# Three-layer graph network and a mixture of experts on one core: the bias products of the experts padded to 128 rows, z loaded back in 13 transfers, the mean negated on Pool

## The reference

```python
x = x + gnn(layernorm(x), edges)          # x is 10000 x 512, 20000 directed edges and loops
x = x + moe(layernorm(x))
# gnn, three layers:
agg = segment_sum(x[src], dst) / max(deg, 1)
out = agg @ Wl + bl + x @ Wr;  x = where(out >= 0, out, a * out)
# moe, 8 experts of 64 hidden columns, the two best of each row:
cw = top2(softmax(x @ Wr + br))
out = sum over e of cw[:, e] * (relu(x @ W1[e] + b1[e]) @ W2[e] + b2[e])
```

## Time and profile before

| | |
|---|---|
| median of 3 runs | 2628.05 us (2627.36 to 2632.61) |
| the profiled execution | 2626.7 us |
| its span | 2624.9 us |
| mean granted clock of TensorE | 0.996 |
| TensorE busy | 2570.3 us (98%) |
| weight loads busy | 1629.7 us (62%) |
| VectorE busy | 1908.0 us (73%) |
| ScalarE busy | 1486.6 us (57%) |
| Pool busy | 1037.5 us (40%) |

### The profile page before, as it was taken

How to read it: one execution, slowest core, us unless ns; L and a number is a source line. 1 busy time by engine, 2 the same in 40 slices (tenths; PEclk the granted TensorE clock), 3 DMA queues, 4 the chain that set the end, 5 groups by cost and what they waited for, 6 DMA issues and landing times.

```text
span 2624.9 us, 40317 instructions
## 1 busy us (share of the span) xinstructions
PE 2570.3 (98%) x9906; PEld 1629.7 (62%) x9906; DVE 1908.0 (73%) x5137; ACT 1486.6 (57%) x3471; POOL 1037.5 (40%) x1291
## 2 busy tenths in 40 slices
PE   7999999999999999999999999999999999999999
PEld 3444445555588865555488874545457777777776
DVE  5555555555699965555599975577579998899996
ACT  2232245555388855555288875555436565556655
POOL 2222245554244445555233325555323333333331
PEclk9999999999999999999999999999999999999999
DMA  4343368887355458888445449988623235223221
GB/s 132 132 134 130 129 206 266 272 267 252 100 165 164 165 186 279 265 270 267 136 152 165 164 155 324 327 283 264 211 73 96 91 93 189 94 87 91 93 89 61
DMA packets 207839, 460.65 MB, mean 175 GB/s; under 512 B 34689, under 2 KB 35001, under 8 KB 207672
## 3 DMA queue, kind: packets, MB, share of 16 engines
q0 software_dynamic: 64928, 207.55, 27.0%
q1 hardware_dynamic: 73480, 124.92, 13.5%
q10 hardware_dynamic: 69264, 126.12, 13.0%
HBM read 245.06 MB, written 213.93 MB: 175 GB/s over the span
## 4 chain that ended last, share of the span: by engine, by line
PE 93%; DVE 2%; DMA 1%; issue 1%; ACT 1%; SPq 0%; POOL 0%; another core or an unknown queue 0%; ACTq 0%; DVEq 0%; POOLq 0%
PE psY L670 11%; PE psY L788 9%; PE psM L788 9%; PE psH L788 8%; PE psY L684 6%; PE psY L692 6%; PE psY L701 5%; PE psT L650 5%; PE psS L800 4%; PE psS L801 4%; PE psY L875 3%; PE psY L878 3%; PE psH L922 3%; PE psH L909 3%; PE psY L887 3%; PE psH L913 3%
## 5 line engine op out<-in xcount | busy, mean ns | idle before, releaser
L559 POOL DMA_INDIRECT rows<-y_rows,lists x471 | 490.7, 1042 | 465.1 <-PE psS L801 304.1
L1323 DVE TENSOR_TENSOR lows<-rows,highs 128x512 fp32r<-128x512 f32 x471 | 326.2, 693 | 354.6 <-ACT highs L956 319.9
L956 ACT ACTIVATE outs<-psS 128x512 f32<-128x512 f32 x471 | 279.6, 594 | 277.2 <-PE psS L801 235.4
L956 ACT ACTIVATE highs<-rows 128x512 fp32r<-128x512 f32 x471 | 294.8, 626 | 144.5 <-ACT outs L956 92.2
L800 PE MATMUL psS<-highs,sel 128*128 128x512 f32 x471 | 346.1, 735 | 11.2 <-ACT outs L956 7.7
L566 POOL DMA_INDIRECT rows<-sum_rows,nodeI x158 | 210.6, 1333 | 314.5 <-DVE rows L1331 299.8
L670 PE MATMUL psY<-wy,res 128*128 128x512 f32 x632 | 285.8, 595 | 0.7 <-ACT res L956 0.7
L956 ACT ACTIVATE outs<-psY 128x512 f32<-128x512 f32 x237 | 141.8, 599 | 223.5 <-PE psY L670 213.7
L788 PE MATMUL psM<-wz,res 128*128 128x512 f32 x544 | 255.5, 592 | 0.0
L788 PE MATMUL psY<-wz,res 128*128 128x512 f32 x536 | 251.7, 592 | 0.0
L788 PE MATMUL psH<-wz,res 128*128 128x512 f32 x528 | 248.0, 592 | 0.0
(11 more groups left out here) (202 smaller groups left out, 4940.6 us busy)
## 6 DMA issues: line engine op xcount, KB each, us to landing
sum_rows<-outs ACTq DMA_DIRECT2D x471, 256.0 KB
y_rows<-outs SPq DMA_DIRECT2D x237, 256.0 KB
rows<-in_x POOLq DMA_DIRECT2D x78, 256.0 KB, 3.0
outs<-in_x SPq DMA_DIRECT2D x78, 256.0 KB
out_rows<-res SPq DMA_DIRECT2D x78, 256.0 KB, 2.0
rows<-y_rows,lists POOLq DMA_INDIRECT x471
z_rows<-res SPq DMA_DIRECT2D x13, 512.0 KB
res<-z_rows SPq DMA_DIRECT2D x1, 6656.0 KB, 24.1
```

The source lines that it names most:

```text
L559: pool.indirect_dma_start(out=rows[:, t % RING, :], out_offset=None, in_=y_d, in_offset=bass.IndirectOffsetOnAxis(ap=col(srcT, t), axis=0) ...
L956: act.activation(o, i_, ACT.Copy).then_inc(signal, 1)
L1323: dve.tensor_tensor(lows[:, t % RING, :], rows[:, t % RING, :], highs[:, g, :].bitcast(F32), ALU.subtract)\
```

## The change

- `twos` and `b1s` get 128 rows. b1 is loaded to all 128 rows by one broadcast transfer instead of two one-row ones. `twos` is one in rows 0 and 1 and zero elsewhere, by way of the new column `two_rows`; `b1s` is zero from row 2 on.
- `cwT` and `b2s` get 128 rows. Pool fills them with zeros once, after the last scatter of the last layer; SyncE's load of b2 and ScalarE's first `norm` wait for it (`pad_set`). Later writes touch rows 0 to 31 alone.
- `bring_back` becomes 13 transfers of two tiles each, one at each k from 30 to 42; piece j waits for j + 1 stores of each of the two slots. VectorE waits for all 13.
- VectorE no longer negates the mean (L1522); Pool's shift becomes mean times reciprocal root times -1 in one operation.

```diff
-        cwT = nc.alloc_sbuf_tensor_at("cwT", [4 * X, 2, P], F32R, offset=lists_at)
+        cwT = nc.alloc_sbuf_tensor_at("cwT", [P, 2, P], F32R, offset=lists_at)
-        twos = nc.alloc_sbuf_tensor_at("twos", [2, P], F32R, offset=res_at + 48 * D + 4 * P)
-        b1s = nc.alloc_sbuf_tensor_at("b1s", [2, D], F32R, offset=res_at + 52 * D)
-        b1raw, b1high = res[0:2, 24, :], res[0:2, 25, :]
+        twos = nc.alloc_sbuf_tensor_at("twos", [P, P], F32R, offset=res_at + 48 * D + 4 * P)
+        b1s = nc.alloc_sbuf_tensor_at("b1s", [P, D], F32R, offset=res_at + 52 * D)
+        b1raw, b1high = res[:, 24, :], res[:, 25, :]
+        two_rows = res[:, 12, 2 * P:2 * P + 1]
-        b2s = nc.alloc_sbuf_tensor_at("b2s", [4 * X, D], F32R, offset=hw_at + 8 * D)
+        b2s = nc.alloc_sbuf_tensor_at("b2s", [P, D], F32R, offset=hw_at + 8 * D)
...
-                for k in range(2):
-                    sp.dma_start(b1raw[k:k + 1, :], b1.rearrange("e f -> (e f)").unsqueeze(0)).then_inc(ex_in, 16)
+                load_row(b1raw, b1.rearrange("e f -> (e f)"), ex_in)
...
                     sp.wait_ge(b2_st, 16)
-                    sp.dma_start(b2s[:, :].bitcast(F32), b2_d).then_inc(b2_back, 16)
+                    sp.wait_ge(pad_set, 2)
+                    sp.dma_start(b2s[0:4 * X, :].bitcast(F32), b2_d).then_inc(b2_back, 16)
...
-            def bring_back():
+            def bring_back(j):
                 for s in range(2):
-                    sp.wait_ge(o_st[s], 16 * (AWAY // 2))
-                sp.dma_start(res[:, AWAY:2 * AWAY, :], z_d.rearrange("(t p) d -> p t d", p=P)).then_inc(z_back, 16)
+                    sp.wait_ge(o_st[s], 16 * (j + 1))
+                a = 2 * j
+                sp.dma_start(res[:, AWAY + a:AWAY + a + 2, :], z_d[a * P:(a + 2) * P].rearrange("(t p) d -> p t d", p=P))\
+                  .then_inc(z_back, 16)
...
-                if k == AWAY + 8:
-                    bring_back()
+                j = k - AWAY - 4
+                if 0 <= j < AWAY // 2:
+                    bring_back(j)
...
+                if l + 1 == LAYERS:
+                    pool.memset(cwT[:, :, :].bitcast(F32), 0.0).then_inc(pad_set, 1)
+                    pool.memset(b2s[:, :].bitcast(F32), 0.0).then_inc(pad_set, 1)
                 pool.wait_ge(mend_st, 32 * (l + 1))
...
-                pool.tensor_tensor(st[:, s, SHIFT:SHIFT + 1], st[:, s, MEAN:MEAN + 1], st[:, s, RSTD:RSTD + 1],
-                                   ALU.mult).then_inc(shift_in[s], 1)
+                pool.tensor_scalar(st[:, s, SHIFT:SHIFT + 1], st[:, s, MEAN:MEAN + 1], st[:, s, RSTD:RSTD + 1], -1.0,
+                                   ALU.mult, ALU.mult).then_inc(shift_in[s], 1)
...
-                copy(cwT[:, s, :], psS[1][0:4 * X, 0:P], cw_sb[s])
+                copy(cwT[0:4 * X, s, :], psS[1][0:4 * X, 0:P], cw_sb[s])
...
             act.wait_ge(mend_add, 2 * LAYERS)
+            act.wait_ge(pad_set, 2)
...
-                dve.tensor_scalar(twos[:, :], iota[0:2, :], 0.0, None, ALU.is_ge).then_inc(ex_set, 1)
+                link(dve.tensor_tensor(two_rows, ident[:, 0:1], ident[:, 1:2], ALU.add))
+                dve.tensor_scalar(twos[:, :], iota[:, :], 0.0, two_rows, ALU.is_ge, ALU.mult).then_inc(ex_set, 1)
...
-                        dve.wait_ge(z_back, 16)
+                        dve.wait_ge(z_back, 16 * (AWAY // 2))
...
-                    dve.tensor_scalar(stat(MEAN), stat(MEAN), -1.0, None, ALU.mult)
```

More of the change, by code:

```diff
@@ L287, in build @@
         cw_made = sem("cw_made")
+        pad_set = sem("pad_set")
         block = ctx.enter_context(nc.Block())
@@ L434, in _ @@
             sp.wait_ge(b2_set, 1)
-            sp.dma_start(b2_d, b2s[:, :].bitcast(F32)).then_inc(b2_st, 16)
+            sp.dma_start(b2_d, b2s[0:4 * X, :].bitcast(F32)).then_inc(b2_st, 16)
             def load_own(k):
@@ L1207, in split_b2 @@
                 link(dve.tensor_scalar(b2raw, b2raw, is_low, None, ALU.mult))
-                dve.scalar_tensor_tensor(b2s[:, :], b2high, is_high, b2raw, ALU.mult, ALU.add).then_inc(b2_set, 1)
+                dve.scalar_tensor_tensor(b2s[0:4 * X, :], b2high, is_high, b2raw, ALU.mult, ALU.add).then_inc(b2_set, 1)
             def carry(k):
@@ L1397, in split_small @@
             def split_small():
-                dve.wait_ge(ex_in, 16 * (X + 3))
+                dve.wait_ge(ex_in, 16 * (X + 2))
                 dve.wait_ge(small_in, 32)
@@ L1403, in split_small @@
                    .then_inc(ex_set, 1)
-                dve.tensor_scalar(twos[:, :], iota[0:2, :], 0.0, None, ALU.is_ge).then_inc(ex_set, 1)
+                link(dve.tensor_tensor(two_rows, ident[:, 0:1], ident[:, 1:2], ALU.add))
+                dve.tensor_scalar(twos[:, :], iota[:, :], 0.0, two_rows, ALU.is_ge, ALU.mult).then_inc(ex_set, 1)
                 link(copy(b1high.bitcast(F32R), b1raw))
                 link(dve.tensor_tensor(b1raw, b1raw, b1high, ALU.subtract))
-                link(dve.tensor_scalar(b1raw, b1raw, ident[0:2, 1:2], None, ALU.mult))
-                link(dve.scalar_tensor_tensor(b1s[:, :], b1high, ident[0:2, 0:1], b1raw, ALU.mult, ALU.add))
+                link(dve.tensor_scalar(b1raw, b1raw, ident[:, 1:2], None, ALU.mult))
+                link(dve.scalar_tensor_tensor(b1s[:, :], b1high, ident[:, 0:1], b1raw, ALU.mult, ALU.add))
                 dve.sem_inc(ex_set, 1)
```

## The result

The changed kernel takes 2568.19 us (median of 4 runs, 2566.55 to 2572.49), the kernel before 2630.33 us on the same chip (2627.36 to 2632.62). The ratio is 0.9768 with a 95% interval of 0.9756 to 0.978. Forecast were 2573 and a range of 2567 to 2586. The profiled executions are 2568.55 and 2626.7 us, 58.2 us apart, where the sum of the prediction said 54.8.

The account below looks back on a forecast made before the run. TensorE, busy 370.00 of 370.00 us, was taken to bound the experts' stage. Padding's 49.4 us plus z's 5.4 made 54.8 us, taking the 2628.05 median to 2573.3, stated as 2573; range 2567 to 2586.

Parts of the forecast that it names:

- the sum of the prediction: Whole kernel: 49.4 us from padding the few-row products plus 5.4 us from splitting the z transfer, 54.8 us less.
- The narrow products: Experts' stage, TensorE: few rows make b1's and b2's products and the groups behind them dearer; padding saves 49.4 us.
- three of four terms: Savings each time: b1 product 0.20, transposes behind 0.15, b2 product 0.19, router behind 0.09 us.
- the place: Rival: surcharge belongs to these products' position in the stream, so padding does nothing and only z helps, 2623; chance 0.04.
- The router behind b2: Four router products behind b2's product fall from 0.54 to 0.45 us, 77 times, 6.9 us.
- VectorE's pace: Experts' stage: VectorE's own tile 7.86 us without the negation, 0.09 under TensorE's 7.95, so TensorE stays the pacer.
- rival 1: Experts' stage: VectorE becomes the bound with a tile of 8.01 us, giving 2579; chance 0.12.
- 0.07 comes off: VectorE's tile in the experts' stage: removing the negation shortens it by 0.07 us, from 7.93 to 7.86.
- z in 13 transfers: Experts' stage near 2220 us: splitting the 6.6 MB transfer removes the late load of x and TensorE's pause, 5.4 us.
- Pool's part: Shift before ScalarE's normalisation comes 0.2 us later, covered by ScalarE's wait before the exponentials; nothing on the path.
- the bound by the eight-column row: Pool's new shift taken as nearest to the same instruction on eight columns, 0.397 us.
- Zeros and b1's broadcast: Pool's clearing (1 us) hides in its scatter wait, b1's 128 rows behind VectorE's waiting; counted nothing, at most 2 us.

Follow-up runs that it names:

- experiments 1: Kernel before with only b1's product padded to 128 rows: 2604.23 us, ratio 0.9917.
- experiment 2: Kernel before with only b2's product padded to 128 rows: 2602.57 us, ratio 0.9913.
- experiment 7: Changed kernel with b1's product on 96 of its 128 rows and b2's on 64: 2598.67 us, ratio to the kernel before 0.9886.
- experiments 6: Changed kernel with b1's product left out, so b1 is not added: 2569.66 us, ratio to the kernel before 0.9777.
- experiment 8: Changed kernel with the addition of eps to the variance moved from VectorE to Pool: 2565.92 us, ratio to the kernel before 0.9765.
- 9: Changed kernel with eps added on Pool and b1's product left out: 2550.92 us, ratio to the kernel before 0.9702.
- Experiment 10: Changed kernel with eps added on Pool, and Pool's gather waiting for VectorE's split of the gates: 2566.54 us, ratio to the kernel before 0.976.
- experiment 3: Kernel before with only the one z transfer cut into 13: 2622.23 us, ratio 0.998.
- 4: Kernel before with only the negation moved from VectorE to Pool's shift: 2628.48 us, ratio 1.0004.

## Why the prediction was right, and where it was off

- **The narrow products.** Right in cause and in three of four terms: 0.20, 0.15 and 0.19 us were measured as 0.20, 0.15 and 0.19. That the row count and not the place is the cause is shown by experiments 1, 2 and 7.
- **The router behind b2** is the mis-sized term: 0.54 - 0.45 = 0.09 was taken, 0.54 - 0.34 = 0.20 measured in experiment 2. The reference form was wrong. The 0.45 was read from router products behind router products; the first one behind a long product costs less. That its weight load is drawn ahead under the long product is how I read the rows of loads (it starts at 2253.27, the router's slot in the chain at 2253.53); it wasn't tried by itself. The load unit's gap in front of it shrank from 0.24 to 0.17 us and didn't go, where the prediction had no idle load unit. The wrong size made 0.11 us a tile, 8 us in all.
- **TensorE's groups of four behind them** (down high, down low, up cross) got dearer by 0.04 us a tile (0.94, 0.92, 0.92), 3 us, which no step had. Why is open. It appears with the b2 padding alone, so neither VectorE's pace nor the z pieces nor the negation bring it. It appears in experiment 7 too, where b2's product reads 64 rows and costs its old 0.42, so the product's shortening doesn't bring it either; what those kernels share is the rest of b2's part, `cwT` and `b2s` with 128 rows and filled once with zeros. TensorE's own tile came to 7.88 instead of 7.95: 8.586 - 0.20 - 0.15 - 0.19 - 0.20 + 0.04 = 7.89.
- **VectorE's pace** was predicted at 7.86, just under TensorE's 7.95, with rival 1 for a VectorE that becomes the bound. Rival 1 came true in kind and not in size: VectorE paces (experiments 6, 8, 9), at 7.91 and not at 8.01, and costs 0.03 us a tile, 2 us, over TensorE's 7.88. The step that failed is "0.07 comes off". With the negation back VectorE ran at 7.923; without it at 7.913, for the cast took 193 ns instead of 168, the split of x 691 instead of 680 and the addition of eps, no longer behind a negation, 154 instead of 144. That is 0.046 of the 0.06 us that are missing. Experiment 10 shows what holds the cast in experiment 8's kernel. That it is the same in the changed kernel is argued, from a tile in which the gather instruction ran from 2302.30 to 2303.45 and the cast ended at 2303.42; the split of x wasn't tried by itself.
- **z in 13 transfers.** Right, 5.4 us against 5.4 (experiment 3).
- **Pool's part.** Counted as nothing and worth nothing (4); the duration was 0.26 instead of 0.4, so the bound by the eight-column row was too high. In the changed kernel it brings 0.010 us a tile, 0.8 us.
- **Zeros and b1's broadcast.** Pool's two memsets took 0.35 and 0.57 us, inside a wait that still lasted 3.41 us behind them: nothing, as forecast. b1's 128 rows were counted as nothing, at most 2 us, because VectorE's waiting would cover them. The bound about held and the nothing did not: the third sum stage is 2.7 us longer in the changed kernel's profile, and on the mean 1.7 longer in the eight kernels with that part (301.0) than in the four without it (299.3).
- **The sum.** 49.4 became 52 (+8 router, -3 groups, -2 VectorE), the pause 5.4, the start of the stage 3.6, and 2.9 us were lost again ahead of the stage, 2.7 of them where b1's rows come in: 58.2 in the profiled pair, 54.8 forecast. That the total is off by only 3 to 5 us is in part luck. Terms that the prediction didn't have, up to 8 us in size, stand on both sides and mostly cancel, and the measured 2568.19 is 1.2 us inside the lower end of the range. TensorE's tile of 7.88 for the forecast 7.95 hides such a pair too, 0.11 off and 0.04 on.

## What to carry to other kernels

A product of few rows in a stream of full ones is dearer than a full one, here 0.43 against 0.23 us, and it charges the group behind it too: count both, and try zeros up to the full height first if the columns stay. The wider operand has a price of its own where it is loaded and prepared, here some 2 us once. When a surcharge is taken away, size what remains from the same form behind the same kind of neighbour, not from the form alone. And when the first engine is relieved by as much as the second one waits, look for the second's pace where it ran freely, and check it by relieving each alone and both together.

## What the runs showed of the hardware

The step in the price lies between 64 and 96 rows: 2, 32 and 64 rows cost 0.42 to 0.43 us, 96 and 128 rows 0.23 (512 columns, granted clock 1.00). A product of 32 output columns in the same stream (the transposes of the gates) cost 0.11 us before and after, and the group behind it 0.93.

A 16-column cast on VectorE took 168 ns, and 292 on the mean where Pool issued a gather at the same time; it then ended 0.02 us before the gather instruction did. The Trainium skill, SBUF — State Buffer, Who interferes with whom, says that VectorE and GpSimd share one pair of ports, that a cast may take the pair, and that the later one is blocked until the first is done; the trace agrees for this cast. The two operations ahead of the cast that ran beside the same gather instruction (L1466 and L1469, each with one of its inputs in PSUM) took their usual 0.68 and 0.69 us.

A big transfer can do its harm far from the place where its data is needed. The transfer of 6.6 MB stood at position 34 of the order and was wanted at 51, and what was late was a 256 KB load of another buffer behind it on the same queue: its issue took 8.42 us, against 0.33 us behind the last of the 13 pieces.
